# Sixteen layers on one core: softplus from ScalarE's own table, GpSimd's C products through the B bank, convolution taps one per slot, and routers that pick by replacing the largest values

## The reference

```python
delta = jax.nn.softplus(jnp.einsum('blr,dr->bld', dt_in, dt_proj_w) + dt_proj_b)
...
def step(h, inp):
    d_t, B_t, C_t, u_t = inp
    dA = jnp.exp(d_t[:, :, None] * A)
    h = h * dA + (d_t * u_t)[:, :, None] * B_t[:, None, :]
    y = jnp.einsum('bdn,bn->bd', h, C_t)
    return (h, y)
```

## Time and profile before

| | us |
|---|---|
| median of 3 runs | 3795.45 (3793.7 to 3796.53) |
| the profiled execution | 3793.41 |
| its span | 3791.6 |
| granted TensorE clock, mean of the span | 0.872 of full speed |

### The profile page before, as it was taken

The page is one execution under the profiler, slowest core; times in us unless marked ns, Lnnn a source line. Parts: engine busy times, 40 slices in busy tenths (PEclk is TensorE's granted clock), DMA queues, the critical chain, the costliest instruction groups (busy, mean ns, idle before and its releaser), DMA issues. The chain is left out here.

```text
span 3791.6 us, 59472 instructions
## 1 busy us (share of the span) xinstructions
PE 3210.3 (85%) x22040; PEld 1706.9 (45%) x22040; DVE 2292.0 (60%) x5886; ACT 1792.3 (47%) x4029; POOL 1035.5 (27%) x412
## 2 busy tenths in 40 slices
PE   7889899897888888889887897888789787788778
PEld 3444444444777777534333342233234333354336
DVE  5666445445666666665589306889841358944991
ACT  3444432424444444343576326777642455633662
POOL 1000000000000000000399105999920106731871
PEclk8999999896555555899899998999999899998999
DMA  4323231120000000022200000000000101140114
GB/s 138 93 84 92 59 104 54 44 82 36 3 3 3 3 3 3 17 76 66 94 0 1 1 0 1 0 1 1 0 0 0 82 1 45 78 184 6 67 81 175
DMA packets 76784, 168.45 MB, mean 44 GB/s; under 512 B 9552, under 2 KB 46544, under 8 KB 67920
## 3 DMA queue, kind: packets, MB, share of 16 engines
q1 hardware_dynamic: 76496, 164.64, 12.9%
HBM read 120.57 MB, written 44.04 MB: 43 GB/s over the span
## 5 line engine op out<-in xcount | busy, mean ns | idle before, releaser
L1204 PE MATMUL psum<-h_ring,h_parts 128*128 128x4 bf16 (+2 forms) x12288 | 418.7, 170 | 123.7 <-ACT h_ring L1285 121.4
L2247 DVE TENSOR_TENSOR_SCAN s_hh<-psum,s_dbu 128x512 f32<-128x512 f32 x384 | 445.5, 1204 | 64.5 <-issue 39.1
L2117 POOL TENSOR_TENSOR s_dbu<-s_du,s_bb 128x1024 f32<-128x1024 f32 x192 | 446.5, 2355 | 53.8 <-ACT s_bb L2002 38.2
L1204 PEld LDWEIGHTS psum<-h_ring,h_parts 128*128 128x128 bf16 x12288 | 372.6, 105 | 174.1 <-ACT h_ring L1285 145.1
L1879 PE MATMUL psum<-s_term,w_c 128*128 128x512 f32 x768 | 381.1, 612 | 0.0
L863 POOL MEMSET r_weights<- 128x512 f32 x4 | 2.1, 524 | 1376.9 <-POOLq L55 922.4
L1285 ACT ACTIVATE h_ring<-h_pre 128x16 f32<-128x16 f32 x1024 | 168.4, 211 | 360.7 <-DVE h_pre L1349 360.6
L2021 ACT ACTIVATE psum<-s_delta,s_decay 128x512 f32<-128x512 f32 x384 | 263.3, 690 | 139.1 <-DVE s_hh L2247 137.7
L1349 DVE TENSOR_REDUCE h_pre<-psum 128x16 f32<-128x48 f32 x1024 | 164.7, 202 | 142.2 <-PE psum L1204 142.2
L872 DVE TENSOR_TENSOR f_hid<-f_gate,psum 128x512 f32<-128x512 f32 x184 | 126.1, 686 | 201.5 <-PE psum L798 193.7
L859 ACT ACTIVATE f_gate<-psum 128x512 f32<-128x512 f32 x184 | 109.7, 597 | 284.6 <-PE psum L794 284.5
(11 more groups left out here) (493 smaller groups left out, 6642.1 us busy)
## 6 DMA issues: line engine op xcount, KB each, us to landing
x_spill<-x_flip SPq DMA_DIRECT2D x28, 1024.0 KB, 3.8
f_share<-f_wide SPq DMA_DIRECT2D x208, 128.0 KB, 3.0
a_ks<-a_spread SPq DMA_DIRECT2D x96, 128.0 KB, 2.8
a_qs<-a_spread SPq DMA_DIRECT2D x96, 128.0 KB, 2.8
x_spare<-x_spill SPq DMA_DIRECT2D x4, 2048.0 KB, 7.7
x_raw<-x_spill SPq DMA_DIRECT2D x4, 2048.0 KB, 7.8
x_norm<-x_spill SPq DMA_DIRECT2D x4, 2048.0 KB, 7.9
w_l3f<-in_l3f SPq DMA_DIRECT2D x1, 7240.0 KB, 20.0
```

The lines of the kernel that those rows point to most:

```text
L1204: mm = nc.tensor.matmul(columns_of(s // BLOCK, grp)[:, s % BLOCK, 0:3 - part, cols], parts[:, part, GROUP * grp + p, :], upper[:, (s - 1) ...
L2117: nc.gpsimd.tensor_tensor(dbu[:, s % 4], du[:, t % 2], both(bb[:, s % B_RING, :]), ALU.mult).then_inc(dbu_ready, 1)
L2247: nc.vector.tensor_tensor_scan(hh[:, s % 4, half, :], DECAYS[i % 3], dbu[:, s % 4, half, :], 0.0, ALU.mult, ALU.add).then_inc(scan_done, 1)
```

## The change

In the scan layers: `BY_POOL` goes from three steps of a turn to five; the C pick of these steps goes through bank `PICK_B`, between B picks; B products run three steps ahead of the scan in a ring of six (before: two in a ring of four); B is picked five steps ahead. Softplus is one ScalarE activation for each half, with a table load before and one after; the second half's rates are computed in `PICK_B`. A convolution's taps are one per slot from slot 17 to 24 instead of four at slots 18 and 22. The first turn's silu of z comes ahead of its dt. In the routers `max_index`, the cast and the one-hots give way to a `match_replace` that puts 3e38 where the picked values are, and one `not_equal`.

```diff
-    for t in range(TILES):
-        last = nc.vector.max_index(at[:, t, :], top[:, t, :], values[:, t, :])
-    link(last)
-    link(nc.vector.tensor_copy(atf[:], at[:]))
-    for k in range(pick):
-        last = nc.vector.tensor_tensor(hot[k][:], g.iota[:, 0:width].unsqueeze(1).broadcast_to([P, TILES, width]),
-                                       atf[:, :, k:k + 1].broadcast_to([P, TILES, width]), ALU.is_equal)
-    link(last)
+    link(nc.vector.memset(top[:, :, pick:8], HIGHEST))
+    for t in range(TILES):
+        last = nc.vector.match_replace(rest[:, t, :], top[:, t, :], values[:, t, :], HIGHEST)
+    link(last)
+    link(nc.vector.tensor_tensor(rest[:], rest[:], values, ALU.not_equal))
...
-    BESIDE = {n: (k + 1,) for k, n in enumerate((3, 6, 9, 10, 11, 12, 14, 16, 17, 18, 19, 20, 22, 24, 26))}
+    BESIDE = {n: (k + 1,) for k, n in enumerate((3, 6, 8, 9, 10, 12, 13, 14, 15, 17, 18, 19, 20, 21, 22))}
...
-    B_RING, B_AHEAD = 6, 4
-    BY_POOL = (3, 8, 13)
+    B_RING, B_AHEAD = 7, 5
+    D_RING, D_AHEAD = 6, 3
+    C_RING = 3
+    BY_POOL = (1, 4, 8, 11, 14)
...
-                    if s in (18, 22):
-                        half = (s - 18) // 4
...
+                    if 17 <= s < 25:
+                        half, late = divmod(s - 17, TAPS)
+                        k = TAPS - 1 - late
+                        if s == 17:
+                            t = b * BR - 2
+                            pe.wait_ge(delta_done, 2 * min(t + 2, TURNS))
+                            if t:
+                                pe.wait_ge(resid_done, t // BR)
+                        if s == 21:
                             pe.wait_ge(conv_kept, 2 * b + 1)
...
+                    if s == 11:
+                        at = (t - 1) * N + 5
+                        pe.wait_ge(b_kept, min(at + B_AHEAD + 1, STEPS))
+                        pe.wait_ge(c_kept, pool_steps(at))
+                        nc.tensor.matmul(PICK_B, w[f"dtw{r}"][:, P:2 * P], dt[0:rank, :], start=True, stop=True).then_inc(rates_ready, 1)
...
-                    if s == 15 and t > 0 and t % BR == 0:
+                    if s == 13 and t > 0 and t % BR == 0:
                         project_out(t // BR - 1)
...
                 def pick_b(s):
                     t, n = divmod(s, N)
+                    at = s - B_AHEAD
...
                     if s:
                         pe.wait_ge(b_kept, s)
+                    if at > 0:
+                        pe.wait_ge(c_kept, pool_steps(at))
+                    if at > 0 and at % N == 6 and at // N + 1 < TURNS:
+                        pe.wait_ge(delta_done, 2 * (at // N + 1) + 2)
...
+                def pick_pool_c(s):
+                    t, n = divmod(s, N)
+                    pe.wait_ge(b_kept, min(s + B_AHEAD + 1, STEPS))
+                    pe.wait_ge(c_kept, pool_steps(s))
+                    nc.tensor.matmul(PICK_B, g.pick_c[0:96, n, :], bc[:, t % 2, :], start=True, stop=True).then_inc(pc_spread, 1)
...
-                    if s in (11, 14):
...
+                    if s == 12:
                         if t >= 2:
                             act.wait_ge(du_done, t - 1)
                             act.wait_ge(da_ready, (t - 1) * 2 * N)
...
+                        for half in range(2):
+                            act.wait_ge(rates_ready, 2 * t + half + 1)
+                            nc.scalar.activation(delta[:, t % 2, half, :], (PRE, PICK_B)[half], ACT.Softplus,
+                                                 bias=w[f"dtb{r}"][:, half:half + 1]).then_inc(delta_done, 1)
+                        nc.scalar.preload_act_table_set("natural_log_exp_and_others")
...
-                times_b(0)
-                times_b(1)
+                for s in range(D_AHEAD):
+                    times_b(s)
                 for s in range(STEPS):
                     t, n = divmod(s, N)
-                    if t + 1 < TURNS:
-                        softplus(t + 1, n)
-                        if n == 13:
-                            inputs(t + 1)
-                    if s + 2 < STEPS:
-                        times_b(s + 2)
+                    if t + 1 < TURNS and n == 7:
+                        inputs(t + 1)
+                    if s + D_AHEAD < STEPS:
+                        times_b(s + D_AHEAD)
                     if s >= 1 and not by_vector(s - 1):
                         times_c(s - 1)
```

More of the change, by code:

```diff
@@ L31 @@
 LOWEST = -3e38
+HIGHEST = 3e38
 class Core:
@@ L624, in _, with chosen @@
                 add_out(CHUNKS - 1)
-def chosen(nc, link, sb, g, name, values, pick, width):
+def chosen(nc, link, sb, name, values, pick, width):
     top = sb(f"{name}_top", [P, TILES, 8])
-    at = sb(f"{name}_at", [P, TILES, 8], U32)
-    atf = sb(f"{name}_atf", [P, TILES, 8])
-    hot = [sb(f"{name}_hot{k}", [P, TILES, width]) for k in range(pick)]
+    rest = sb(f"{name}_rest", [P, TILES, width])
     for t in range(TILES):
@@ L730, in vector @@
         link(tt(group[:, :, 0:4], best[:], next1[:], ALU.add))
[L731 to L734 removed]
+        _, g1 = chosen(nc, link, sb, "r_g", group[:], 2, 8)
+        quads = lambda x: x[:].rearrange("p t (q a) -> p t q a", a=4)
+        link(tt(quads(biased), quads(biased), g1[:, :, 0:4].unsqueeze(3).broadcast_to([P, TILES, 4, 4]),
                 ALU.mult))
[L736 to L739 removed]
+        _, hot = chosen(nc, link, sb, "r_e", biased[:], 4, 16)
+        link(tt(weights, scores[:], hot[:], ALU.mult))
         link(nc.vector.tensor_reduce(total[:], weights, AX.X, ALU.add))
@@ L780, in gated_experts @@
         flat = sb("r_flat", [P, CHUNK])
-        router.e = sb("r_exp", [P, TILES])
+        router.e = sb("r_exp", [P, TILES, 8])
         with nc.Block() as block:
@@ L1673, in selective_scan @@
         through = sb("s_through", [P, 2, P])
-        down = sb("s_down", [P, 1])
         neg = sb("s_neg", [64, 64], BF16)
@@ L1774, in row_part @@
                     xs = fixed(g.normed, b)
-                    if s in (18, 22):
-                        half = (s - 18) // 4
-                        if half == 0:
-                            pe.wait_ge(norm.normed, b + 1)
-                        if half:
-                            pe.wait_ge(conv_kept, 2 * b + 1)
-                        elif b:
-                            pe.wait_ge(mag_kept, 2 * min((b - 1) * BR if BR == 2 else b, TURNS))
-                            if b * BR >= 3:
-                                pe.wait_ge(resid_done, (b * BR - 2) // BR)
-                        for k in reversed(range(TAPS)):
-                            late = TAPS - 1 - k
-                            mm = nc.tensor.matmul(PRE[:, late:], w["taps"][:, (2 * k + half) * P:(2 * k + half + 1) * P], xs[:, 0:CHUNK - late],
-                                                  start=(late == 0), stop=(k == 0))
-                        mm.then_inc(conv_ready, 1)
+                    if 17 <= s < 25:
[7 more added lines that the diff above has]
+                        if s == 21:
+                            pe.wait_ge(conv_kept, 2 * b + 1)
+                        mm = nc.tensor.matmul(PRE[:, late:], w["taps"][:, (2 * k + half) * P:(2 * k + half + 1) * P], xs[:, 0:CHUNK - late],
+                                              start=(late == 0), stop=(k == 0))
+                        if k == 0:
+                            mm.then_inc(conv_ready, 1)
                     if s in (26, 29):
@@ L1909, in _ @@
                         add_up(s - 3, 1)
-                    if s < STEPS:
+                    if s < STEPS and by_vector(s):
                         pick_c(s)
+                    elif s < STEPS:
+                        pick_pool_c(s)
                 project_out(CHUNKS - 1)
@@ L2004, in keep_c @@
                 def keep_c(s):
-                    act.wait_ge(c_spread, s + 1)
-                    if pool_steps(s) >= 2:
-                        act.wait_ge(term_pool, pool_steps(s) - 1)
-                    nc.scalar.copy(cc[:, pool_steps(s) % 2, :], PICK_C).then_inc(c_kept, 1)
+                    act.wait_ge(pc_spread, pool_steps(s) + 1)
+                    if pool_steps(s) >= C_RING:
+                        act.wait_ge(term_pool, pool_steps(s) - C_RING + 1)
+                    nc.scalar.copy(cc[:, pool_steps(s) % C_RING, :], PICK_B).then_inc(c_kept, 1)
                 def decays(s, half):
@@ L2205, in _ @@
-                first_grow(0)
-                first_grow(1)
-                first_sum(0)
-                first_part(0)
-                first_sum(1)
-                first_part(1)
-                dve.wait_ge(f_delta, 1)
-                dve.wait_ge(delta_done, 1)
-                u_there(dve, 0)
-                nc.vector.tensor_tensor(du[:, 0], delta[:, 0], u[:, 0], ALU.mult).then_inc(du_done, 1)
+                for half in range(2):
+                    u_there(dve, 0)
+                    dve.wait_ge(delta_done, half + 1)
+                    mm = nc.vector.tensor_tensor(du[:, 0, half, :], delta[:, 0, half, :], u[:, 0, half, :], ALU.mult)
```

200 lines of the change are left out of this document (49 added, 151 removed).

## The result

| | before | after |
|---|---|---|
| median, us | 3795.05 (4 runs) | 3734.88 (3734.15 to 3735.96, 4 runs) |
| the profiled execution | 3793.41 | 3734.15 |
| its span | 3791.6 | 3732.4 |

The ratio is 0.9842, with a 95% interval of 0.9825 to 0.9859: 60.2 us less. The forecast was 69 less, 3726, with 3734.9 inside its range. The page's busy line answers to the earlier trace rows: VectorE and GpSimd lose 45 and 38 us of work, TensorE hardly any.

What follows compares the result with a forecast made beforehand. VectorE and GpSimd, both nearly full, wait for each other in different parts of a scan turn. Stage two -49.3 and stage one -19.8 give -69.1 us: 3793.4 becomes 3724.3, median 3726, range 3700 to 3757.

Steps and rivals of the forecast that it cites:

- the softplus block: ScalarE's softplus with its table loads: VectorE stalls 1.3 us per block, +9.1 us in stage two, +3.9 in stage one.
- the taps: Convolutions with one tap per slot on TensorE: 3.4 us of stall each for 5.1; -3.7 and -2.2 us.
- silu: ScalarE's silu block, with step 14 moved to GpSimd: VectorE's stall 1.42 becomes 2.6; +0.6 and +0.2 us.
- C products: Two more steps per scan turn on GpSimd: VectorE saves 18.9 us in stage two and 9.4 in stage one.
- GpSimd's softplus: Softplus operations leave GpSimd, so VectorE's scan waits for late B products go: -29.2 and -9.9 us.
- Starts: Scan stage starts: first scan sooner, -7.0 us in stage two, -5.2 in stage one, where 3.0 go again.
- Ends: End of each scan stage: with step 14 on GpSimd the last additions finish sooner, -1.7 us per stage.
- Routers: Expert-stage routers: VectorE's shorter chain lies under TensorE's gate and up matmuls, so no time changes.
- Rival 3: ScalarE drains 1.28 us more at each of 20 new table loads, uncovered: +26 us, 3752; chance 0.06.
- Rival 1: Scan turns follow GpSimd's pace alone, 51.0 us, the three-step lead hiding VectorE's stalls: 3685; chance 0.14.
- Rival 2: Part of the 39 us of scan waits was not softplus, or convolutions stay whole: 3752; chance 0.12.
- Rival 4: Shared bank makes TensorE wait for ScalarE's copies at GpSimd steps: mild 3756, chance 0.07; decisive 3822, chance 0.06.

Runs made afterwards that it cites:

- e9: Changed kernel with three C products per turn on GpSimd (steps 3, 8, 13) instead of five, softplus still on ScalarE: 3765.1 us.
- e5: Changed kernel with B products two steps ahead in a ring of four, instead of three in a ring of six: 3738.1 us.
- e10: Kernel before the change with five C products per turn on GpSimd and its softplus left as it was: 3811.6 us.
- e1: Changed kernel with Exp for Softplus in every turn but the first, without the two table loads; computes something else: 3738.7 us.
- e12: Changed kernel with Exp for Silu of u and z in later rows, without the two table loads; computes something else: 3726.4 us.
- e3: Changed kernel with four convolution taps of a half together in slots 18 and 22 instead of one per slot: 3733.7 us.
- e6: Changed kernel with TensorE's first matmuls of the next turn's vectors one slot later (slot 1 instead of 0): 3735.9 us.
- e11: Changed kernel with one tap per half instead of four in the later rows' convolutions; does not compute the reference: 3717.9 us.
- e4: Changed kernel with VectorE's C products at half width in every turn but a stage's first; computes something else: 3727.0 us.
- e2: Changed kernel with two more decay buffers, in SBUF, and decays made two steps ahead instead of one: 3882.3 us.

## Why the prediction was right, point by point

**Total.** From first scan to step 14 of the last turn 4.2 us are missing (0.2 in stage two, 4.0 in stage one), at the two ends 3.3, in the starts 1.2; some 1.2 lie elsewhere. That is the 9.9 between -69.1 and -59.2 of the span. The sum came out so near in part because errors of its terms cancel: the softplus block (+13) and the late projection (+3) cost nothing, while the taps (-5.9) brought nothing and silu cost more than its +0.8.

**C products, -28.3: nearly right.** VectorE's busy time fell by 18.7 in stage two, forecast 18.9. Taken away alone (e9) the products are worth 17.9 and 6.1 in stage lengths, 24.0 for 28.3.

**GpSimd's softplus, -39.1: the reason is right, the size is not isolated.** No scan waits for "issue" any more, nor with three C products (e9) or the old lead (e5), and e10 shows it from the other side: while GpSimd keeps softplus, more C products on it make the kernel slower. No run puts softplus back by itself. What e9 gives is everything but the C products: 26.8 us in the windows of the earlier trace rows, which become 234.8 and 442.2, where the prediction's other terms sum to 25.2.

**Softplus block, +13: wrong, it costs nothing (e1).** The step that failed is the cover at softplus, 5.8 us of chain against 4.6 of VectorE's work with 1.3 of stall left over. The block was sized right (3.9 us) but all ten show 0.25 of stall. And a stall of VectorE counted one for one, which it does not in a turn whose pace GpSimd sets.

**Silu, +0.8: mis-sized, and mis-added.** VectorE's waits for decays in stage two before:

```profile
2330.76 1.22 DVE L2247 TENSOR_TENSOR_SCAN s_hh<-psum,s_dbu 128x512 f32<-128x512 f32 x1 [2.98 <-ACT psum L2021]
2377.43 2.34 DVE L2247 TENSOR_TENSOR_SCAN s_hh<-psum,s_dbu 128x512 f32<-128x512 f32 x2 [1.42 <-ACT psum L2021]
2498.15 2.34 DVE L2247 TENSOR_TENSOR_SCAN s_hh<-psum,s_dbu 128x512 f32<-128x512 f32 x2 [1.42 <-ACT psum L2021]
2617.68 2.34 DVE L2247 TENSOR_TENSOR_SCAN s_hh<-psum,s_dbu 128x512 f32<-128x512 f32 x2 [1.42 <-ACT psum L2021]
```

The 7.2 of the earlier trace rows hold 2.98 from the stage's start, and only 4.3 at the three blocks. So "7.2 becomes 7.8" compares unlike sums: five blocks at 1.42 becoming 2.6 are +5.9 by the prediction's own rule. Measured is 3.59 in place of 1.42 five times, 10.9 of stall. e12 shows that about half of such a stall reaches the turn.

**Taps, -5.9: wrong, 0 (e3).** The step that failed is 3.4 us in place of 5.1 per convolution. The same passes have to fit between the same picks, and one per slot TensorE still waits 1.26 us for the first half's copy. The forecast 3.4 of stall per convolution was close (3.5); it was the comparison with 5.1 that was not: with the taps together in the changed kernel (e3), no wait of that length appears at a convolution (there stand 0.39 before a C product and 1.31 before a scan), so the taps' standing together does not by itself make 5.1. What else made it was not tried. VectorE's waits before C products, other than for its own scans, sum in stage two to 12.8 after (7.1 and 5.7) against 12.5 before (11.8 and 0.7).

That stage two's window came out within 0.2 us is in part luck: the taps' 3.7 did not come, but waits for decays grew by 8.0 where silu and softplus were to bring 9.7 (silu brought 6.5 and softplus 1.8), and no wait for the late output projection (+1.5) shows.

**Stage one, 4.0 too little.** There a gate falls in each turn with a convolution, and the forecast VectorE turn of 48.8 had no gate in it. The two such turns take 58.5 and 60.5, which is 1.7 and 2.1 more than the first and the later of their kind in stage two (56.8 and 58.4). In each VectorE's gate waits 0.8 and a C product of GpSimd's behind it 1.7. That is as large as what is missing, but the slip at silu is a rival for 2.2 of it (two blocks of 1.18 where the sum has 0.2); no run tells them apart.

**Starts, -7.0 and -5.2: right.** From stage one's last addition to stage two's first scan 6.7 us less; stage one's first scan 4.3 earlier, in a stage that began 0.8 later.

**Ends, -1.7 each: 0.1 in this run, right where the clock held.** The prediction let all of TensorE's queue run at full clock, as the earlier trace rows shows it. With no next turn to prepare TensorE stood 3.10 us ahead of step 14; then its granted clock was 0.52, and the additions took 3.48 instead of 1.88. That puts GpSimd's C pick 1.6 us later, which is the whole term. No run was made for this, but other traces show both cases with the same code: in both stages of e12, stage two of e1 and stage one of e6 and of e11 the clock fell about 9 us before the pick for step 14 and was full again by then, TensorE stood 1.4 to 1.6 us ahead of that pick, the additions took 1.88, and the end was 13.0 us. Before the change it is 14.8.

**Routers, 0: right.** From the weights' clearing on GpSimd to TensorE's turn of them it is 45.3 us before and after, in the stage of the earlier trace rows; in the other three it changes by -0.2, -0.1 and +1.1. The 1.1 goes with TensorE's clock (0.86 granted there for 0.89), and in e9, with the same router, that stage takes 30.2 us for 30.1 before.

**The table switch.** The load takes 1.28 and the next activation starts 1.30 after its start, at softplus as at silu; e12 takes two loads away and the block becomes 2.7 shorter, 1.35 each. The Trainium skill ("ScalarE: Activation LUTs", What ACT_TABLE_LOAD costs) has a drain of 1.38 on top of 1.28; the measurements do not show it. Rival 3 falls.

**Rival 1** was half right. GpSimd's pace alone sets the turns without a convolution, at 50.9 for its forecast 51.0 (e4). But not by the third step of lead (e5), and the turns with a convolution it does not set. **Rival 2** falls for the scan waits; for the convolutions it holds, since the spread of the taps brings nothing. **Rival 4** falls: at the shared bank TensorE waits for copies 5.0 us before picks in all of stage two, 1.3 at the most, and 5.3 before the rates.

## What to carry to other kernels

When two engines are both nearly full and each waits for the other, first take work off the one in whose bursts the other stands, and only then shift work onto it: the same shift of two products a turn cost 15 us in the kernel before and brought 30 in the changed one. A stall of VectorE cost nothing in the turns that GpSimd paces (e1) and about half its length in those with a convolution (e12); read the pace of one period of each kind before pricing stalls, and test it by making one engine's work lighter (e4), which is a cheaper and clearer answer than removing waits one by one. Spreading the taps over TensorE's slots moved waits but did not shorten the stages (e3).

## What the runs showed of the hardware

- A scan of 128x512 that reads both inputs from SBUF while GpSimd works takes 2.45 us on average, up to 3.4; with one input in PSUM 1.20 (e2). The shortest with both inputs in SBUF takes 1.19, so it is not the place of the input alone. GpSimd's products grow from 2.35 to 2.80 in the same stretch. The Trainium skill ("SBUF — State Buffer", SBUF: two separate sides) has this: a VectorE operation with two SBUF inputs and GpSimd lock each other out for a whole instruction. The numbers agree with it: 3.4 is 1.2 plus 2.2, nearly one operation of GpSimd's.
- After 3.10 us without work TensorE was granted 0.52 of its clock, the lower of its two levels (1.2 GHz), for some 3.5 us; at the same place before the change its longest wait was 1.61 and the clock stayed at 1.00. The length of the last wait does not tell it alone: in the changed kernel four passes behind a wait of 2.03 (at 2708.41) took 1.88, and in e9 two passes behind one of 2.03 (at 2719.07) took 1.67 instead of 1.02. The price at the end of a stage is 1.7 us between otherwise equal ends (14.7 and 13.0), and it can hide or give back as much in a comparison of two runs.
- Softplus is one activation of 0.68 us for 128x512, as Exp from a decay is (0.69), and it has its own table load of 1.28.
